# Second attention of a fused two-layer kernel: the load of a later group's queries, keys and values is issued ahead of the store of shares

## What is computed

```python
qkv = (x @ w_qkv).reshape(B, T, 3, H, hd)            # H = 8 heads of 32, causal
scores = jnp.einsum('bhqd,bhkd->bhqk', q, k) * scale
scores = jnp.where(causal[None, None], scores, -jnp.inf)
scores = scores + head_scales[None, :, None, None] * geo
attn = jax.nn.softmax(scores, axis=-1)
out = jnp.einsum('bhqk,bhkd->bqhd', attn, v).reshape(B, T, C)
return out @ w_out
```

## Time and profile before

| | |
|---|---|
| median of 3 runs | 1914.5 us (1914.3 to 1917.1) |
| profiled execution | 1909.37 us, span 1907.4 us |
| TensorE busy over the span | 94% |
| VectorE | 75% |
| ScalarE | 59% |
| GpSimd | 28% |
| mean granted TensorE clock | 0.961 of 2.4 GHz |
| DMA | 239.18 MB, mean 125 GB/s; SyncE's queue 36.8% of the 16 engines' span |
| second attention | from about 1127 to 1545 us of the span |

### The profile page before, as it was taken

How to read it: one execution, slowest core, us unless ns; L and a number is a source line. 1 busy time by engine, 2 the same in 40 slices (tenths; PEclk the granted TensorE clock), 3 DMA queues, 4 the chain that set the end, 5 groups by cost and what they waited for, 6 DMA issues and landing times. The chain is left out here.

```text
span 1907.4 us, 34604 instructions
## 1 busy us (share of the span) xinstructions
PE 1795.9 (94%) x12690; PEld 1170.9 (61%) x12690; DVE 1429.7 (75%) x2814; ACT 1117.3 (59%) x2212; POOL 528.6 (28%) x686
## 2 busy tenths in 40 slices
PE   8989999999999999799999989999999987999994
PEld 4545444444444444388888865555555566999994
DVE  7879999999999999367677655466666554766665
ACT  4645888888888888622333214446463632655555
POOL 5760000233000001032223212212525243444444
PEclk9986999999999999899999988999999998999997
DMA  4883744565434502023444255546666334655555
GB/s 170 280 260 53 124 79 96 131 144 122 86 57 73 83 28 85 20 76 111 153 143 147 89 188 120 137 100 156 153 154 156 97 107 147 150 144 144 145 115 196
DMA packets 146600, 239.18 MB, mean 125 GB/s; under 512 B 25830, under 2 KB 81159, under 8 KB 146449
## 3 DMA queue, kind: packets, MB, share of 16 engines
q1 hardware_dynamic: 113312, 171.48, 36.8%
q0 software_dynamic: 17024, 34.25, 7.0%
q10 hardware_dynamic: 16112, 31.46, 4.5%
HBM read 137.49 MB, written 96.60 MB: 123 GB/s over the span
## 5 line engine op out<-in xcount | busy, mean ns | idle before, releaser
L994 DVE TENSOR_REDUCE b_mx<-b_PM 128x1 f32<-128x512 f32 x1024 | 621.0, 679 | 17.9 <-PE b_PM L848 17.5
L970 ACT ACTIVATE b_probs<-b_PS 128x512 f32<-128x512 f32 x1000 | 523.9, 606 | 69.1 <-PE b_PS L902 53.8
L848 PE MATMUL b_PM<-b_kst,b_qst 48*128 48x512 f32 x888 | 280.9, 430 | 0.0
L2919 ACT ACTIVATE d_probs<-d_PS 128x512 f32<-128x512 f32 (+3 forms) x384 | 166.5, 496 | 183.2 <-PE d_PS L2822 182.5
L902 PE MATMUL b_PS<-b_qst,b_kst 50*128 50x512 f32 x744 | 256.9, 436 | 2.1 <-issue 0.2
L2958 DVE TENSOR_REDUCE d_mx<-d_PM 128x2 f32<-128x1024 f32 (+1 forms) x192 | 179.9, 950 | 101.5 <-PE d_PM L2774 59.3
L902 PEld LDWEIGHTS b_PS<-b_qst,b_kst 50*128 50x128 f32 x744 | 120.4, 184 | 163.4 <-ACT b_probs L970 147.4
L2874 POOL TENSOR_SCALAR_AFFINE_SELECT d_probs<-d_probs 128x128 f32<-128x128 f32 x256 | 74.6, 305 | 268.1 <-ACT d_probs L2919 263.4
L790 POOL CAST b_mhalves<-b_maxima 128x16 fp32r<-128x16 f32 x32 | 6.3, 197 | 505.3 <-DVE b_maxima L1003 505.3
L848 PEld LDWEIGHTS b_PM<-b_kst,b_qst 48*128 48x128 f32 x888 | 142.0, 184 | 5.4
L874 PE MATMUL b_PO<-b_probs,x_v 128*32 128x384 f32 (+2 forms) x2048 | 145.2, 390 | 0.0
(11 more groups left out here) (318 smaller groups left out, 3753.9 us busy)
## 6 DMA issues: line engine op xcount, KB each, us to landing
halves<-a_parts SPq DMA_DIRECT2D x7, 2048.0 KB, 8.7
qk<-c_halves ACTq DMA_DIRECT2D x7, 2048.0 KB
w_w<-L_ffn_fc1T SPq DMA_DIRECT2D x12, 1024.0 KB, 5.0
w_w<-L_ffn_fc2T SPq DMA_DIRECT2D x12, 1024.0 KB, 6.3
b_qst<-halves SPq DMA_DIRECT2D x72, 128.0 KB, 4.4
b_kst<-halves SPq DMA_DIRECT2D x72, 128.0 KB, 7.6
d_qst<-qk SPq DMA_DIRECT2D x36, 256.0 KB, 5.2
d_kst<-qk SPq DMA_DIRECT2D x36, 256.0 KB, 7.4
```

The costliest lines, as they stand in the source:

```text
L848: mm = pe.matmul(PM[n % MBANKS][:], qst[buf][at, p, first:first + P], kst[buf][at, p, kh * BLK:(kh + 1) * BLK], start=True, stop=True)
L970: act.activation(probs[:, s % RING], score_bank(g, s)[:], ACT.Exp).then_inc(exped, 1)
L994: dve.tensor_reduce(mx[:, half, (r * PAIRS0 + p) * TPH + t, kh:kh + 1], PM[n % MBANKS][:], AX.X, ALU.max)\
L2919: act.activation(probs[:, s % RING, 0:w], PS[bank(s)][:, 0:w], ACT.Exp).then_inc(exped, 1)
```

## The change

In SyncE's loop over the groups the load of group g+3, with its wait on `pv_done`, moves up: it stood behind `store_shares(g - 1, 1)`, `sums(g, 0)`, `rows(g + 1)` and `load_shares(g - 1, 1)`, and now stands behind `load_shares(g - 1, 0)` and in front of those four. Nothing is added or taken away.

```diff
--- before.py
+++ after.py
@@ -2724,17 +2724,18 @@
                 if g > 0:
                     sums(g - 1, 1)
                     route.load_shares(sp, d, g - 1, 0)
+                if g + BUFS - 1 < GROUPS:
+                    if g > 0:
+
+                        sp.wait_ge(pv_done, g * ROUNDS + RING // G1)
+                    load(g + BUFS - 1)
+                if g > 0:
                     route.store_shares(sp, d, g - 1, 1)
                 sums(g, 0)
                 if g + 1 < GROUPS:
                     rows(g + 1)
                 if g > 0:
                     route.load_shares(sp, d, g - 1, 1)
-                if g + BUFS - 1 < GROUPS:
-                    if g > 0:
-
-                        sp.wait_ge(pv_done, g * ROUNDS + RING // G1)
-                    load(g + BUFS - 1)
                 if g == GROUPS - 3:
                     route.wait_sums_free(sp, BATCH - 2)
                     weights.load_up(sp, d, bass.ds(0, 1), 0)
```

## The result

The changed kernel takes 1964.4 us (median of 4 runs, 1949.2 to 1968.2), the kernel before beside it 1915.8 (4 runs): ratio 1.023, 95% interval 1.018 to 1.028. The profiled execution is its fastest, 1949.21 us; its span is 39.9 us above that of the earlier trace rows.

The account below looks back on a forecast made before the run. TensorE was taken as nearly always busy, the change touching only its waits for transfers. -15.0 + 14.2 + 3 + 6 = +8.2 us gave 1914.5 + 8.2 = 1922.7 us for the median, range 1903 to 1936.

Parts of the forecast that it names:

- the landing of the rows, load + 16: Rows of minus the maxima land 16 us after the load's start in groups 1 to 3, 16.4 in 7 and 11.
- the price of the waits that hangs on it: TensorE waits for rows in slot 0 after groups 1, 2, 3, 7 and 11, 2.8 to 2.9 us each: 14.2 us.
- The gain, -15.0: All four TensorE waits for keys, in groups 2, 3, 8 and 12, go: 15.0 us at most.
- The mechanism: On SyncE's queue, totals and rows now stand behind the 2 MB load, are issued and land later, and TensorE waits.
- each of the three signs: Rows waits 1.5 to 3.2 us; first sums pair taking 4 us or more; slot 10 inversions waiting 2 to 4 us.
- one of the signs of being wrong: Periods of groups 4, 8 and 12 above 23.8 and 27.6 us would point to VectorE as the bound.
- Groups 5, 6, 9 and 10 hide it: These groups reach slot 0 later than 20 us into their period, so the late rows cost nothing there.
- The clock, 1.2 us each: TensorE's clock falls behind five new stalls, 0 to 2.5 us each, taken as 1.2: 6 us.
- Groups 4, 8 and 12, 1 us each: Late totals and shares hold VectorE in these groups, 0 to 3 us each, taken as 1: 3 us.
- The first (in time anyway): Small transfers still arrive in time, slot 0 waits for nothing: faster, 1899.5 to 1909.5 us; chance 0.20.
- the second (a draw): Rows land at load + 14.7 to 15.2 and the clock stays up: within 4 us of 1914.5; chance 0.22.
- The third, VectorE as the bound: Late totals and shares hold VectorE 3 us in groups 4, 8, 12; clock falls each stall: +22, 1936 us; chance 0.10.

Follow-up runs that it names:

- the half load in the old place: Kernel before with every load issued from group 1 on cut to 1 MB, part of the attention working on stale data: 1899.9 us, ratio 0.992.
- the second part of experiment 1: Kernel before with only the rows of minus the maxima issued by GpSimd on its own queue in slot 7: 1909.6 us, ratio 0.998.
- fills: Changed kernel with identity products on TensorE ahead of the wait for rows in groups 2, 3, 4, 7, 8 and 12: 1959.7 us, ratio 1.022.
- experiment 2: Changed kernel with the load one place later, behind the store of shares, still ahead of sums and rows: 1964.5 us, ratio 1.026.
- experiment 1: Changed kernel with only the rows of minus the maxima issued by GpSimd on its own queue in slot 7: 1950.2 us, ratio 1.019.
- 4: Changed kernel with rows (slot 7) and totals of half 0 (slot 6) issued by GpSimd on its own queue: 1941.9 us, ratio 1.016.
- experiment 3: Kernel before with only the queries (three DMAs, 768 KB) sent early, keys and values in the old place: 1921.5 us, ratio 1.005.

## Why the prediction was right in sign and too small

The forecast was +8.2 us; the median moved by +48.6 (1964.4 - 1915.8), the spans of the profiled executions by +39.9. The way and the kind of wait were right; the step that failed is the landing of the rows, load + 16, with the price of the waits that hangs on it: in five of seven groups they land 18.8 to 20.1 us after the load's first issue. Step by step:

- **The gain, -15.0: right.** No wait for keys is left, and in the half load in the old place, without waits for keys as well, groups 2, 3, 8 and 12 take 15.1 us less than in the kernel before. That the 3.8 us of groups 8 and 12 are the worth of their waits for keys is not shown: in the second part of experiment 1 they lose 4.7 and 2.6 us without any, while VectorE waits.
- **The mechanism: right.** The first score product of a group waits for the rows, the totals pair takes 4.5 to 8.5 us to issue in the seven groups in which it does, inversions in slot 10 wait 2.6 to 7 us in six of them: each of the three signs came, two of them larger than named. So did one of the signs of being wrong, a group 4 above 23.8 (26.0).
- **The landing, load + 16 to 16.4: the term that failed.** It fits groups 1 and 3 (16.5, 16.1). In the others it is 20.0 (group 2), 20.1 (6), 18.8 (7), 19.4 (10) and 19.7 (11). What is late is the issue: the sum had SyncE free of the blocked pair of totals at load + 10.1; it is free of it at 9.8 and 10.4 in groups 1 and 3, and at 12.5 to 14.6 in the other five. The rows follow, and land 3.6 to 5.4 us after their own issue. I took the term from loads that had the engines nearly to themselves; where the load now starts it meets 1 MB of GpSimd's: tokens (issued 1205.71, 1315.30, 1427.74: groups 2, 6, 10) or the routing's store (1342.60, 1453.13: groups 7, 11). That this is what parts the five groups from the other two is read from the times; no run takes that traffic away. It could have been read in the trace of before: the load of group 1 starts at 1188.75 there, GpSimd issues the tokens at 1198.43, and the store of shares behind the load has landed only at 1208.22, 19.5 us after the load's first issue:

```profile
1198.43 1.11 POOL L1817 DMA_DIRECT2D e_x<-x  x2
...
1208.22 0.57 SPq L1810 DMA_DIRECT2D w_w<-shares  x1
```

The late landing makes waits of 5.2, 6.3 and 7.4 us in groups 2, 7 and 11, where 2.8 to 2.9 stood.

- **"Groups 5, 6, 9 and 10 hide it": wrong for 6 and 10.** A landing at load + 20 leaves 3.05 and 0.77 us bare. Together the waits for rows are 30.0 us in seven groups, not 14.2 in five.
- **The clock, 1.2 us each: too small.** The seven groups lose 42.2 us over clean ones, 12.2 beyond their idle time: 1.7 each, and 12.2 where the sum had 6. With fills the price behind one stall was 2.3; that all 12.2 are the clock's is not shown.
- **Groups 4, 8 and 12, 1 us each: too small.** 2.2, 3.2 and 3.3, 8.7 where the sum had 3. Groups 8 and 12 contain a wait of 2.4 to 2.5 us for ScalarE's copy of the maxima; its cause stays open, and it is absent from the second profile of the changed kernel, where the three groups lose 1.2 us together and the groups behind them 15.4.
- **The sum again:** -15.2 (before's loss) + 42.2 + 8.7 + 0.8 (groups 5, 9, 13) = 36.5.
- **The rivals.** The first (in time anyway) and the second (a draw) fell: no landing was under 16 us. The third, VectorE as the bound, had a mechanism that is real but hardly shows in the profiled execution; in the one of 1957.0 us groups 5, 9 and 13 take 14.5 us more than in the first and groups 4, 8 and 12 take 7.5 less, so it accounts for part of what lies between the profile and the median. Its time of 1936 was still too low, for it had the same 15.4 for the rows. The range ended at 1936 for that reason: its upper bound took 16.4 us as the longest landing, and not the 19.5 of a load beside other traffic.

**The hold-up and the slower transfer.** In the changed kernel most of the lateness is the late issue: the rows land 3.6 to 5.4 us after it, against 3.5 in the kernel before. Curing the issue alone does not cure the landing: not held up (experiment 2), or on GpSimd's queue (1 and 4), the rows of group 1 take 6.9, 8.1 and 8.3 us, and land 12.8 to 13.7 us after the load's first issue instead of 16.5. Both parts shrink when the bytes go.

What holds the issue is not the number of DMAs in front alone. In experiment 2 SyncE issues 14 DMAs in 7.7 us from 1184.41 on, the load among them, and none is held up; there the store of shares goes ahead of the load. In the attention, in all 14 profiles together, SyncE has 56 rows (of one to three DMAs) that take 4 us or more to issue. Each time the DMA just ahead is a store of shares, as at 1186.17 above. Whether that store has a part in it stays open: no run takes it away.

## What to carry to other kernels

A load may be issued as early as its buffer allows only if no small transfer that an engine needs soon is sent while it is in flight; ask of each place in the queue which small transfers start while the load is in flight (some 12 us for 2 MB here), on every queue, and when each is needed. Taking them off the load's queue brought back 0.2 to 0.7 points of the 2.1 to 2.3 here, and halving the bytes all of it; where several small transfers are late together, curing one uncovers the next. When a landing time is read from the trace of before, check what else the DMA engines carry at the new moment, not at the old.

## What the runs showed of the hardware that I had not expected

**Issuing is held up across queues.** With the load on GpSimd's queue, SyncE's two totals DMAs took 4.8 and 6.8 us to issue in groups 1 and 2 instead of 1.2; with the load on SyncE's own, 4.5 and 8.1 us in the changed kernel, and up to 9.9 in experiment 1. With the store of shares ahead of the load (experiment 2) they took 1.2.

**The clock can fall with TensorE busy.** In experiment 3, group 6, no weight load waited for a transfer, TensorE was busy for 17.8 of 18 us, and the clock still was at its lower level for 13.7 us:

```profile
1303.00:1306.00 3.00, 2.98 (x21) 2.50 (x20) 1.29 (x2) 1.09 (x2) 0.20 (x1) 1.00 0.94 308
1306.00:1309.00 3.00, 2.82 (x13) 1.60 (x13) 1.27 (x3) 1.19 (x2) 0.00 (x0) 0.56 1.07 245
1309.00:1312.00 3.00, 3.00 (x15) 2.59 (x12) 0.90 (x5) 0.14 (x1) 0.00 (x0) 0.50 0.49 107
...
1318.00:1321.00 3.00, 3.00 (x13) 1.08 (x9) 0.00 (x0) 0.52 (x2) 0.00 (x0) 0.66 0.49 118
```

It cost some 6 us (31.0 against 24.7 for the group), and came again in group 14 there, in group 6 of the half load in the old place (31.0) and in group 14 of the changed kernel run again (28.8 against 23.1). What sets it off was not found; it is a part of the spread of single executions, and a reason to read a difference of 6 us in one profile with care.
